# Two hardware loops of the expert part written out as straight programs

## The reference

```python
def _L0_ffn_ref(input, Wg, W1, b1, W2, b2):       # E = 8, D = 128, H = 256, TOP_K = 2
    probs = jax.nn.softmax(jnp.einsum('bsd,de->bse', input, Wg), axis=-1)
    top_vals, top_idx = jax.lax.top_k(probs, TOP_K)
    top_vals = top_vals / jnp.sum(top_vals, axis=-1, keepdims=True)
    onehot = jax.nn.one_hot(top_idx, E, dtype=input.dtype)
    mask = jnp.sum(onehot, axis=2)
    scores = jnp.sum(onehot * top_vals[..., None], axis=2)
    xm = input[None] * jnp.moveaxis(mask, -1, 0)[..., None]
    h = jax.nn.relu(jnp.einsum('ebsd,edh->ebsh', xm, W1) + b1[:, None, None, :])
    y = jnp.einsum('ebsh,ehd->ebsd', h, W2) + b2[:, None, None, :]
    return jnp.sum(y * jnp.moveaxis(scores, -1, 0)[..., None], axis=0)
x = x + _layernorm(_L0_attn_ref(_layernorm(x), ...))
x = x + _layernorm(_L0_ffn_ref(_layernorm(x), ...))
```

## Time and profile before

| what | value |
|---|---|
| median of 3 runs | 1102.99 us (1102.98 to 1104.02) |
| the profiled execution's own time | 1101.95 us |
| its span, first to last instruction | 1099.9 us |
| PE, DVE, ACT, POOL busy, share of the span | 93%, 84%, 60%, 56% |
| granted TensorE clock, mean | 0.978 |

### The profile page before, as it was taken

One profiled execution on the slowest core, in us unless ns is written; L12 is line 12 of the kernel. 1 busy time (PEld: TensorE's weight loads), 2 busy tenths in 40 slices (PEclk: granted clock), 3 DMA queues, 4 the chain that ended last, 5 costly groups with the idle time before them and its releaser, 6 DMA issues.

```text
span 1099.9 us, 27462 instructions
## 1 busy us (share of the span) xinstructions
PE 1023.0 (93%) x9060; PEld 862.7 (78%) x9060; DVE 920.0 (84%) x2590; ACT 654.5 (60%) x1237; POOL 620.6 (56%) x873
## 2 busy tenths in 40 slices
PE   4899999999999999999997689998989898989996
PEld 2687777778777777778776578887979797979885
DVE  6768887888888878888786768998989898989987
ACT  5778788878878787878774233443434343434441
POOL 6346665666556665667545525555555454545654
PEclk9999999999999999999998889999999999999998
DMA  6000000000000000000003000000000000000000
GB/s 187 4 4 4 3 4 4 4 2 5 4 5 2 3 4 5 2 3 4 4 4 98 1 1 11 11 11 10 10 10 10 10 3 8 10 11 10 10 11 20
DMA packets 19614, 14.53 MB, mean 13 GB/s; under 512 B 4360, under 2 KB 16928, under 8 KB 19488
## 3 DMA queue, kind: packets, MB, share of 16 engines
q1 hardware_dynamic: 19488, 13.02, 4.3%
HBM read 7.77 MB, written 4.19 MB: 11 GB/s over the span
## 4 chain that ended last, share of the span: by engine, by line
PE 57%; DVE 21%; issue 11%; ACT 4%; SPq 2%; DMA 2%; POOL 1%; DVEq 1%; POOLq 0%; ACTq 0%
PE bank L1576 12%; PE bank L751 6%; PE bank L548 4%; DVE moe_acc L1625 4%; PE bank L823 3%; PE bank L550 3%; PE bank L1549 3%; PE bank L549 3%; PE bank L1550 3%; PE bank L1551 3%; PE bank L735 3%; DVE moe_h L1427 3%; PE bank L737 2%; PE bank L769 2%; PE bank L806 2%
## 5 line engine op out<-in xcount | busy, mean ns | idle before, releaser
L1560 ACT ACTIVATE moe_hid<-bank,moe_b 128x512 f32<-128x512 f32 x256 | 168.3, 687 | 185.7 <-PE bank L1551 185.1
L1576 PEld LDWEIGHTS bank<-moe_w,moe_hid 128*128 128x128 f32 x2048 | 249.1, 193 | 22.6 <-ACT moe_hid L1560 6.1
L1576 PE MATMUL bank<-moe_w,moe_hid 128*128 128x128 f32 x2048 | 251.6, 276 | 6.8 <-DVE moe_acc L1625 5.7
L1625 DVE SCALAR_TENSOR_TENSOR moe_acc<-bank,moe_scores,moe_acc 128x128 f32<-128x128 f32 x448 | 125.6, 342 | 39.6 <-PE bank L1576 31.6
L1549 PE MATMUL bank<-moe_t_hi,moe_w_hi 128*128 128x512 f32 x256 | 114.8, 448 | 0.0
L1602 POOL TENSOR_TENSOR moe_b_mix<-moe_b_mix 128x512 f32<-128x512 f32 x80 | 107.6, 1345 | 10.2
L548 PE MATMUL bank<-thi,whi 128*128 128x512 f32 x224 | 104.6, 467 | 6.1 <-DVE tlo L670 2.5
L835 ACT ACTIVATE m<-bank 128x512 f32<-128x512 f32 x128 | 69.6, 595 | 65.2 <-PE bank L737 65.0
L919 DVE TENSOR_TENSOR mg<-bank,m 128x512 f32<-128x512 f32 x128 | 82.4, 686 | 26.0 <-PE bank L751 25.5
L1550 PE MATMUL bank<-moe_t_lo,moe_w_hi 128*128 128x512 f32 x256 | 103.7, 405 | 0.0
L1551 PE MATMUL bank<-moe_t_hi,moe_w_lo 128*128 128x512 f32 x256 | 102.7, 401 | 0.0
(11 more groups left out here) (180 smaller groups left out, 2511.6 us busy)
## 6 DMA issues: line engine op xcount, KB each, us to landing
out_dram<-moe_outb SPq DMA_DIRECT2D x16, 256.0 KB, 2.3
parts<-csplit SPq DMA_DIRECT2D x128, 4.0 KB
rows<-csplit SPq DMA_DIRECT2D x128, 4.0 KB
moe_w<-in_L_ffn_W_dram SPq DMA_DIRECT2D x1, 1024.0 KB, 5.5
m<-in_L_attn_w_in_proj_dram SPq DMA_DIRECT2D x1, 772.0 KB
xall<-in_L_attn_hidden_dram SPq DMA_DIRECT2D x2, 256.0 KB, 3.7
moe_b<-in_L_ffn_b_dram SPq DMA_DIRECT2D x1, 512.0 KB, 9.4
mg<-n_L_attn_w_out_proj_dram SPq DMA_DIRECT2D x1, 128.0 KB, 2.4
```

Source lines behind the costliest of these rows:

```text
L1560: SE.activation(hid[:, e % 2, n, :], up_banks[k % 4][:], ACT.Relu, bias=b1[:, k:k + 1]).then_inc(hid_ready.sem, 1)
L1576: mm = PE.matmul(bank[:, col(i)], hid[:, e % 2, n, col(i)], w2[:, e, n, :], start=n == 0, stop=n == FB - 1, skip_group_check=True)
L1625: DVE.scalar_tensor_tensor(out=acc[:, par, i, :], in0=y, scalar=s, in1=acc[:, par, i, :], op0=ALU.mult, op1=ALU.add).then_inc(acc_step.sem, 1)
```

## The change

In `over_groups` the hardware loop becomes a loop of the program that writes the kernel, so b is a number, the slices are static, and the six passes stand one behind the other on PE, ACT, DVE and POOL. SP's loop over its stores is written out in the same way. No operation on data is added, removed or put elsewhere.

```diff
     def over_groups(eng, body):
         for u in range(2):
             body(eng, 0, u, static, u == 0, False)
-        with eng.Fori(1, GROUPS // 2 - 1) as b:
+        for b in range(1, GROUPS // 2 - 1):
             for u in range(2):
-                body(eng, b, u, dynamic, False, False)
+                body(eng, b, u, static, False, False)
         for u in range(2):
             body(eng, GROUPS // 2 - 1, u, static, False, u == 1)
...
         for u in range(2):

             sp.nop(nofuse=True).then_inc(stored[u], 1)
-        with sp.Fori(0, GROUPS // 2) as b:
+        for b in range(GROUPS // 2):
             for u in range(2):
                 g = 2 * b + u
                 sp.wait_ge(out_ready.sem, out_ready.of(g))
-                sp.dma_start(ov[:, bass.ds(g * TG, TG), :], outb[:, u, :, :]).then_inc(stored[u], 16)
+                sp.dma_start(ov[:, g * TG:(g + 1) * TG, :], outb[:, u, :, :]).then_inc(stored[u], 16)
         for u in range(2):
             sp.wait_ge(stored[u], 1 + 16 * GROUPS // 2)
```

## The result

The changed kernel takes **1117.06 us** (median of 4 runs, 1110.98 to 1120.44) against 1102.99 for the kernel before (4 runs, 1098.23 to 1104.02): a ratio of 1.0112, 95% interval 1.0061 to 1.0163. The forecast was 1115.0, in the range of 1094 to 1120. So writing the loops out costs 14 us, although five stalls of 2.9 us are gone. The profiled execution took 1117.32 us.

A forecast was written before the change was run, and what follows sets the result against it. PE and DVE were both nearly full, so neither bounds alone. Twelve groups at 29.09 us plus seven low clocks at 1.57 gave +10.7, the tail +1.3: +12.0 on 1101.95, or 1113.95; median 1115.0 us, range 1094 to 1120.

The forecast's parts named there:

- Step 1: DVE at the loop's back edge: five gaps of 2.90 us go, 14.5 us of DVE time.
- Step 2: POOL's run of eleven operations: gaps fall from 0.14 to 0.08 us, so it ends 1.3 us sooner per group.
- Step 3: DVE beside POOL: fewer instructions slip into shorter gaps; four L1674 rise from 2.97 to 4.97 us, L1427 from 1.84 to 4.09.
- Step 4: One group, mark to mark: DVE waits 0.87 us, L1427 is caught again, and the state repeats at 29.09 us.
- Step 5: PE behind its turn's wait: 3.4 us at half clock, 1.57 us more (30.66 a group), in seven of twelve groups.
- The sum: Twelve groups cost +10.7 us, the last two groups +1.3: +12.0, giving 1113.95 profiled and 1115.0 median.
- Step 6: SP, ACT and instruction fetch: nothing else changes the time; no cost taken for fetch in straight code.
- Rival 1: DVE and POOL: a faster lasting cycle, two L1427 slipping through, 28.38 us a group, 1094.2 us; chance 0.22.
- Rival 2: DVE's back edge: only the branch counts, the 14.5 us come back whole, 1088.5 us; chance 0.05.
- Rival 3: PE's turns: the forecast's cycle of 29.09 us a group without the low clock, 1104.0 us; chance 0.11.

The follow-up runs named there:

- run 1: The changed kernel with only POOL's hardware loop kept, DVE, PE, ACT and SP straight: 1080.63 us, ratio 0.9775.
- run 2: The kernel before with only POOL's loop (and SP's) written out, the other engines keeping theirs: 1132.38 us, ratio 1.0258.
- run 3: The changed kernel with a nop put back between POOL's operations in all groups, without register or branch: 1067.80 us, ratio 0.9654.
- run 4: The changed kernel with ten extra matmuls that nobody reads ahead of PE's turn: 1097.45 us, ratio 0.9947.
- run 5: The changed kernel with five extra additions on DVE, read by nobody, once in group 2: 1115.32 us, ratio 1.0098.
- run 9: The kernel before with only SP's loop of stores written out: 1102.47 us, ratio 0.9984.
- run 6: The changed kernel with DVE's normalisation (L1427) moved ahead of the addition for expert 1: 1084.19 us, ratio 0.9802.

## Why the prediction was right, point by point

- *Step 1, the branch.* Right: no gap of 2.9 us at L1625 is left.
- *Step 2, POOL's gaps.* Right: 0.08, and 13.55 to 13.58 us in groups 1 to 14.
- *Step 3, what DVE gets of them.* Right in size and cause: 4.97 and 4.09, and runs 1 and 2 switch both numbers by POOL's program alone, run 3 by its nops alone. That two instructions get in at a gap of 0.14 and one at 0.08 is seen in the single L1674 shown in run 3.
- *Step 4, the cycle.* Right: DVE's wait behind the mark is 1.00 (forecast 0.87), the turn waits 2.04, and a group without low clock takes 29.08 (forecast 29.09). Run 4 holds it for twelve groups.
- *Step 5, the clock.* The price was right: 30.65 a group with the low clock (30.66), 1.57 against 1.55 measured. The number of groups was **mis-sized**: I took four in seven from the earlier trace rows, seven of twelve, and it was twelve of twelve in one profile and ten in the other. The term was 7.85 us too small. In the kernel before PE's waits vary in length and place from group to group; in the changed one they are alike, and so was what followed 25 of the 28 in the two profiles. So a share counted over unlike waits was a poor chance for equal ones. Longer waits were not followed more often: of the five of 2.91 to 2.92 in the kernel before, two were, and of the four in run 5 from 0.92 to 2.70, none. What decides for a single wait stays open.
- *The sum.* With twelve low groups my own number was 1123, and it came to 1117. The twelve groups gave the +18.5 that this case has. The rest came out lower. Up to the mark at 689.78 the kernel after was 1.76 us ahead of the earlier trace rows, 1.55 of it ahead of group 1's mark, where the code is the same: chance. From the mark of group 14 to the end it took 57.87 us against 59.02, -1.15 where I had put +1.3. In that tail group 14 did cost +1.34 (29.08 against 27.74). But group 15 took 23.22 against 24.82: PE's wait of 1.81 in it was followed by a low clock in the kernel before (at 1082.36) and not in the one after. A wait of 1.80 or 1.81 stands at this place in ten of the twelve profiles, and four were followed by one, so this too I count as chance. The last 0.9 lies behind the last L1674 (3.68 us to the end of the span against 2.78), where only the last store is left. So 12.0 + 7.85 - 1.76 - 2.45 = 15.6. For the profiled execution I had 1113.95 and it took 1117.32, 3.4 us more. The median came nearer, because the first profile had lain 1.04 below its median and the second lay 0.26 above. That the forecast lies 2 us from the median is partly luck, with errors that cancel: the mechanism was right, the count of low groups wasn't.
- *Step 6.* Right for SP (run 9). Fetch shows no gap in DVE's straight code either.
- *Rival 1* decided as described, at DVE's wait behind the mark, but run 5 refutes it as a state that lasts. Its sum was right for one group (28.48 against 28.38) and had no term for PE's second wait of 0.87, which I take for what ends it; no run takes that wait away. *Rival 2* would hold only with POOL's gap kept, and run 1 shows that it then gains even more than 14.5 us (23), in part since the low clock goes too: the twelve groups gained 21.2 us, and two low-clock stretches of the kernel before make up some 3 of them. The sentence of the Trainium skill, Runtime: NRT & Kernel Launch, Instruction fetch mechanics, that kernels prefer full unrolling fits the branch, as the gaps of 2.9 us went with it. Taken alone it gives the wrong sign for this kernel, whose ratio was 1.0112. *Rival 3* is run 4's state: 29.10 a group and 1097.45, below the 1104.0 that I gave, because time fell outside the twelve groups too: group 2's mark came 2.4 us earlier than in the earlier trace rows (689.14; group 1 had no low clock either) and the end 1.1 us sooner behind the mark of group 14.

## What to carry to other kernels

Before a loop is written out, look at which engine's gaps it closes: here the idle 0.06 us between GpSimd's operations, put there by a nop, was worth more to the kernel than five branches of 2.9 us. Where a VectorE group in SBUF takes a multiple of its usual time beside a long GpSimd run, try a nop between the GpSimd operations (1117 to 1068 us) and try moving the VectorE group ahead of that run (to 1084), and then both (1055). When each group of a periodic schedule has the same short wait of TensorE, price the low clock for all of them as well, not for a share alone: 25 of 28 had it here.

## What the runs showed of the hardware

- Eleven nops a group on POOL, one ahead of each big operation, lengthen its run from 13.6 us to between 14.6 and 14.9 and shorten the kernel by 49 us (1117.06 to 1067.80).
- Between two POOL operations with a gap of 0.08 us one waiting DVE instruction got in, with a gap of 0.14 two did, the second in 0.34 us (the single L1674 in run 3).
- A wait of 2.04 us in PE that is otherwise without a pause was followed by 3.4 us at 1.2 instead of 2.4 GHz in 13 of 14 cases in one profile and 12 of 14 in the other, and never when ten matmuls filled it: 1.55 us a group, 1117.06 to 1097.45 in all. Of the waits of 1.26 to 1.28 us in run 6, one a group, none was followed so.
- In run 1's loop, with targets worked out from a register, POOL's run starts 1.73 us behind the mark against 1.41 in straight code. The nop isn't the reason: in run 3, with nops and no registers, it is 1.40 (740.20 less the mark at 738.80).
